# Tile-wise last unit, smaller first loads and later weight splits in a fused two-layer graph kernel

## Chip, cores and metric

The kernel runs on one NeuronCore of a Trainium2 chip. The metric is the device time of one execution in microseconds. Lower is better. Names of engines: PE is TensorE, DVE is VectorE, ACT is ScalarE, POOL is GpSimd, SP is SyncE (here it only issues transfers).

## What is computed

128 graphs of 64 nodes with 384 features pass through two blocks, each followed by a residual sum and a LayerNorm without weights.

```python
x = layernorm(x + attention(x, adj))      # 12 heads of 32; softmax((q k^T)/sqrt(32) + beta*adj), masked where adj <= 0
x = layernorm(x + digcn(x, adj))          # two inner layers l = 0, 1:
#   u = h h^T / sqrt(384);  delta = softmax(u) * adj;  attn = delta / (sum(delta) + 1e-10)
#   ctx = (attn*upper) @ (h Wl + bl) + diag(attn) * (h Ws + bs) + (attn*lower) @ (h Wr + br)
#   h   = relu(layernorm(ctx) * ln_w + ln_b)
```

## The kernel before

**Tiles and units.** A unit is 256 nodes, that is two tiles `t` of 128 nodes, each with two graphs. There are 32 units. Every product with a 384x384 weight is made in three passes of TensorE: both factors are split into a high part (`*_hi`, rounded by ACT) and a low part (`*_lo`, the rest, by DVE or POOL), and `product` (lines 359 to 361) issues high*high, low*high and high*low. So each input of a projection needs two small steps, one on ACT and then one on DVE, before TensorE can start.

**Pipeline.** The program is a loop of steps. In a step three units are in work: EARLY (projections v, q, k and the scores), MID (softmax, attention output, first outer norm, giving `h0` and its transpose `hT`) and LATE (both inner layers). A fourth stage, FINAL, finishes the second inner norm, the sum with `h0` and the last norm of the unit that was LATE one step ago. Each engine has its own instruction list, and the order in it is written out by hand in a `step` function per engine. Engines wait for one another through semaphores only, and each one executes its list in order, so that an instruction that waits holds up everything that is written behind it.

**One LATE unit on PE.** `gram` (u of both tiles), `project_sides` (four projections LEFT and RIGHT for two tiles), `transpose_e`, `project_self` twice, `mix` (the context sums). Layer 0's context is then normalized by DVE, POOL and ACT, and `transpose_z` brings it back for layer 1, which repeats all of it. Between `mix(st, 0)` and `transpose_z` the step puts the EARLY unit's v, q and k projections; between `transpose_z` and `gram(st, 1)` it puts `transpose_probs`, `project_qk(st, 2)` and `attend`. For the last two units there is no EARLY unit left, and for the last one no MID unit either.

**Tile granularity.** In layer 0 and 1 both tiles go together: `make_ctx` writes both tiles' contexts, `stats_inner` takes both tiles' statistics, `inverse_root` on POOL makes both scale factors by one instruction of 128x2, and so on up to `normalize` and the store of a unit's 384 KB of output.

**Beginning.** SP issues x of unit 0 as one load of 384 KB, then three loads of 384 KB with slice m of both w_q and w_k, then the rest. ACT splits x (line 651), then the six weight parts (line 628), DVE the same (lines 830 and 838), and PE makes the three `project_qk`. Until then PE runs ten warm-up products on the identity (line 558). `take_qk` on ACT (lines 660 and 662) moves q and k of a slice out of one PSUM bank; both lie in the same bank. `scores` (line 428) waits for all six. ACT splits the w_v parts between the first and the second `take_qk`.

**Weights of layer 1.** Weights 6, 7 and 8 are split by ACT at the end of `second` (line 641) and by DVE (line 851) in the first step that has a LATE unit: 6 and 7 before `mask_scores`, 8 after `mask_aT`.

## Time and profile before

| what | us |
|---|---|
| median of 3 runs (range) | 1292.63 (1292.51 to 1294.82) |
| the profiled execution | 1295.08 |
| its span, first to last instruction | 1293.4 |
| PE busy in the span | 1261.8 (98%) |
| DVE, ACT, POOL busy | 984.8, 629.7, 366.7 |
| mean granted TensorE clock | 0.990 of full |

The span is 1.7 us shorter than the execution's own time, since it leaves out what lies before the first and after the last instruction. The chain of work that ended last is 96% PE. In the 40 slices of the page PE stands at 9 tenths or more in 36, and is lower in the first and in the last three, which is where the change works.

### The profile page before, as it was taken

How to read it: one execution, taken by the hardware profiler on the slowest of the kernel's cores; microseconds unless marked ns; L12 is line 12 of the kernel's file. 1: busy time of each engine (PE TensorE's matmuls, PEld its weight loads, DVE VectorE, ACT ScalarE, POOL GpSimd, SP SyncE). 2: the span in 40 equal slices, each digit the busy share in tenths (PEclk: the TensorE clock that was granted, in tenths of full speed). 3: DMA queues.
4: the chain of work that ended last, by engine and by line, in shares of the span. 5: the costliest groups of instructions: out<-in, count | busy, mean ns of one | idle time of the engine just before them, and what ended most of it. 6: DMA issues, size and time to landing. Idle time of an engine off the chain costs nothing.

```text
span 1293.4 us, 34503 instructions
## 1 busy us (share of the span) xinstructions
PE 1261.8 (98%) x13844; PEld 1168.9 (90%) x13844; DVE 984.8 (76%) x2672; ACT 629.7 (49%) x1329; POOL 366.7 (28%) x398
## 2 busy tenths in 40 slices
PE   8999999999999999999999999999999999999885
PEld 8999999999999999999999999999999999999774
DVE  5777778777778777878777878777878777787765
ACT  5544554544554544554534554445545445545432
POOL 3222323322323232323222323222323222323211
PEclk9999999999999999999999999999999999999997
DMA  8211111011110111110111110111110111110000
GB/s 273 82 40 57 57 57 30 29 56 57 57 57 24 35 56 57 57 57 18 41 57 56 57 57 7 51 57 57 57 49 9 57 57 57 57 35 12 26 13 25
DMA packets 52206, 66.32 MB, mean 51 GB/s; under 512 B 17744, under 2 KB 38352, under 8 KB 51920
## 3 DMA queue, kind: packets, MB, share of 16 engines
q1 hardware_dynamic: 52048, 64.12, 16.3%
q8 instruction: 110, 1.80, 0.6%
q14 instruction: 48, 0.39, 0.1%
HBM read 38.54 MB, written 12.58 MB: 40 GB/s over the span
## 4 chain that ended last, share of the span: by engine, by line
PE 96%; DVE 2%; issue 1%; ACT 1%; POOL 0%; DMA 0%; POOLq 0%; ACTq 0%; SPq 0%; DVEq 0%
PE bank L359 25%; PE bank L361 23%; PE bank L360 23%; PE bank L550 7%; PE bank L462 4%; PE bank L499 4%; PE bank L447 3%; PE bank L428 3%; PE bank L475 2%; PE bank L485 2%; PE bank L530 1%; DMA late<-in_w_qk 0%; DVE ln_six L1012 0%; DVE probs L900 0%; POOL probs L1184 0%
## 5 line engine op out<-in xcount | busy, mean ns | idle before, releaser
L359 PE MATMUL bank<-w_hi,hT_hi 128*128 128x384 f32 x1158 | 405.2, 350 | 1.9 <-DVE hlr L966 1.0
L361 PE MATMUL bank<-w_hi,hT_lo 128*128 128x384 f32 x1158 | 390.3, 337 | 0.0
L360 PE MATMUL bank<-w_lo,hT_hi 128*128 128x384 f32 x1158 | 390.1, 337 | 0.0
L359 PEld LDWEIGHTS bank<-w_hi,hT_hi 128*128 128x128 f32 x1158 | 218.4, 189 | 6.6 <-issue 2.2
L360 PEld LDWEIGHTS bank<-w_lo,hT_hi 128*128 128x128 f32 x1158 | 219.0, 189 | 0.0
L361 PEld LDWEIGHTS bank<-w_hi,hT_lo 128*128 128x128 f32 x1158 | 218.5, 189 | 0.0
L966 DVE TENSOR_TENSOR hlr<-bank,rows 128x384 f32<-128x384 f32 x256 | 142.0, 556 | 79.4 <-PE bank L361 76.6
L1197 POOL TENSOR_TENSOR ln_rstd<-ln_var,minus_half 128x2 f32<-128x2 f32 x128 | 98.7, 771 | 350.6 <-DVE ln_var L1018 131.5
L1184 POOL TENSOR_TENSOR probs<-probs,row_max 128x768 f32<-128x768 f32 x64 | 94.3, 1475 | 275.9 <-DVE row_max L906 275.9
L981 DVE TENSOR_TENSOR late<-bank,rows 128x384 f32<-128x384 f32 x128 | 71.3, 557 | 123.5 <-PE bank L361 123.5
L359 PE MATMUL bank<-xT_hi,w_hi 128*128 128x256 f32 x558 | 158.8, 285 | 0.0
L360 PE MATMUL bank<-xT_lo,w_hi 128*128 128x256 f32 x558 | 156.1, 280 | 0.0
L361 PE MATMUL bank<-xT_hi,w_lo 128*128 128x256 f32 x558 | 155.9, 279 | 0.0
L722 ACT ACTIVATE late<-late,diag 128x384 f32<-128x384 f32 x64 | 39.5, 618 | 225.4 <-DVE late L981 225.4
L1161 POOL TENSOR_TENSOR xT_lo<-xT_in,xT_hi 128x768 fp32r<-128x768 f32 x31 | 57.6, 1857 | 229.6 <-ACT xT_hi L651 229.6
L715 ACT ACTIVATE e_di<-bank,u_bias 128x128 f32<-128x128 f32 x128 | 45.9, 363 | 132.8 <-DVE u_bias L945 132.8
L361 PEld LDWEIGHTS bank<-xT_hi,w_lo 128*128 128x128 f32 x558 | 106.2, 190 | 0.0
L359 PEld LDWEIGHTS bank<-xT_hi,w_hi 128*128 128x128 f32 x558 | 104.8, 188 | 0.1
L360 PEld LDWEIGHTS bank<-xT_lo,w_hi 128*128 128x128 f32 x558 | 104.9, 188 | 0.0
L550 PE MATMUL bank<-hlr,aT 64*64 64x386 f32 x1024 | 97.8, 497 | 0.0
L730 ACT ACTIVATE late<-late,diag 64x384 f32<-64x384 f32 x128 | 78.4, 613 | 36.1 <-DVE late L981 30.4
L737 ACT ACTIVATE h<-h,ln_shift,ln_rstd 128x384 f32<-128x384 f32 x64 | 41.9, 702 | 99.7 <-DVE ln_shift L866 99.7
(101 smaller groups left out, 2349.0 us busy)
## 6 DMA issues: line engine op xcount, KB each, us to landing
v_halves<-v_stage SPq DMA_DIRECT2D x128, 99.0 KB, 2.3
xT_in<-in_xT SPq DMA_DIRECT2D x32, 384.0 KB, 3.5
x_in<-in_x SPq DMA_DIRECT2D x32, 384.0 KB, 4.1
out<-late SPq DMA_DIRECT2D x32, 384.0 KB, 2.4
late<-in_w SPq DMA_DIRECT2D x7, 576.0 KB, 5.7
adj_in<-in_adj SPq DMA_DIRECT2D x32, 96.0 KB, 3.9
adjT_in<-in_adjT SPq DMA_DIRECT2D x64, 48.0 KB, 3.2
rows<-in_vectors SPq DMA_DIRECT2D x1, 1536.0 KB, 8.0
```

The source lines that it names most:

```text
L359: nc.tensor.matmul(o, l_hi, r_hi, start=first and n == 0, stop=False)
L360: nc.tensor.matmul(o, l_hi, r_lo, start=False, stop=False)
L361: done = nc.tensor.matmul(o, l_lo, r_hi, start=False, stop=final and n == last)
L462: done = nc.tensor.matmul(o[g * N:(g + 1) * N, h:h + 3:2, :], pT[:, t * PAIRS + j, g * N:(g + 1) * N], v[:, :, j, :], start=True, stop=True)
L499: done = nc.tensor.matmul(U_BANK[l][g * N:(g + 1) * N, t * N:(t + 1) * N], a, a, start=kc == 0, stop=kc == KC - 1)
L550: done = nc.tensor.matmul(CTX_BANKS[l][t][o * N:(o + 1) * N, 0:MW], aT[rows_of, t, m, rows_of], hlr[rows_of, t, m, 0:MW], start=m == LEFT, ...
L730: nc.scalar.activation(self_turned[o * N:(o + 1) * N], h_self[rows_of, 1], ACT.Copy, scale=diag[rows_of, 1:2]).then_inc(self_scaled, 1)
L966: nc.vector.tensor_tensor(hlr[:, t, m, 0:D], HLR_BANKS[l][2 * t + m][:, 0:D], bias_row[l][m], ALU.add).then_inc(hlr_ready, 1)
L981: nc.vector.tensor_tensor(h_self[:, t], SELF_BANKS[l][t][:, 0:D], bias_row[l][SELF], ALU.add).then_inc(self_ready, 1)
L1161: nc.gpsimd.tensor_tensor(xT_lo[:, :, :], xT_in[:, slot], xT_hi[:, :, :].bitcast(F32), ALU.subtract).then_inc(xlo_ready, 1)
L1184: nc.gpsimd.tensor_tensor(s, s, row_max[:, t * H:(t + 1) * H].unsqueeze(2).to_broadcast([P, H, N]), ALU.subtract).then_inc(s_shifted, 1)
L1197: nc.gpsimd.tensor_tensor(rstd[:, :], var[:, :], minus_half[:, :], ALU.pow).then_inc(s_rstd, 1)
```

## The change

It has three parts, and two buffers that they need.

1. Beginning. x of unit 0 is loaded in three loads of 128 KB, w_q and w_k in six of 192 KB. The first of the six is issued from ACT's queue, the other eight loads from SP's. ACT and DVE split each part as it lands, in the order x0, q0, x1, x2, k0, q1, k1, q2, k2. PE's first q product waits for one third of x at a time. k of the last slice goes to bank 6 instead of sharing bank 3 with q, and `take_qk` waits for q and for k apart. The split of w_v moves behind the second `take_qk`.
2. Weights 6, 7 and 8. On ACT their splits move from the end of `second` into the next step, behind `exp_gram`, and x's split stands between 7 and 8. On DVE they move behind `mask_scores`: 6 ahead of the third and 7 ahead of the fourth `sides_bias`. This is a move in the first step with a LATE unit alone.
3. The last two units get orders of their own. `next_to_last` puts `transpose_probs` and `attend` ahead of `transpose_z` on PE, and rearranges DVE, ACT and POOL. `last` handles unit 31 tile by tile: own PSUM banks, tile-wise normalization, transposes, split in pieces of 128x128, gram, statistics, POOL factors, last norm and store; its FINAL stage is in the same step. Two changes of storage make it possible: `h0` has three slots instead of two, and the layer 1 context has two buffers instead of one.

The order on ACT at the start, before (hT_hi is the high part of x here, late holds the raw weights, 3x128 elements is one weight part, qT and kT are the `take_qk` moves):

```order
L651 ACT_TABLE_LOAD
L651 ACTIVATE hT_hi<-xT_in 128x768
L628 ACTIVATE w_hi<-late 128x3x128 x6
L637 ACTIVATE columns<-columns 128x3
L660 ACTIVATE qT<-bank,columns 128x256
L662 ACTIVATE kT<-bank,columns 128x256
L633 ACTIVATE w_hi<-late 128x384 x3
L660 ACTIVATE qT<-bank,columns 128x256
L662 ACTIVATE kT<-bank,columns 128x256
L660 ACTIVATE qT<-bank,columns 128x256
L662 ACTIVATE kT<-bank,columns 128x256
```

and the same engine and place after:

```order
L837 ACTIVATE hT_hi<-xT_in 128x256
L843 ACTIVATE w_hi<-late 128x3x128
L837 ACTIVATE hT_hi<-xT_in 128x256 x2
L843 ACTIVATE w_hi<-late 128x3x128
L852 ACTIVATE columns<-columns 128x3
L843 ACTIVATE w_hi<-late 128x3x128 x2
L877 ACTIVATE qT<-bank,columns 128x256
L880 ACTIVATE kT<-bank,columns 128x256
L843 ACTIVATE w_hi<-late 128x3x128 x2
L877 ACTIVATE qT<-bank,columns 128x256
L880 ACTIVATE kT<-bank,columns 128x256
L848 ACTIVATE w_hi<-late 128x384 x3
```

The x split is in three, the weight parts stand between the moves, and the three splits of w_v (the last row) have moved behind the second pair of moves; the third pair follows.

On PE in the step of unit 30, from the layer 0 `mix` (hlr, aT) to the layer 1 `gram` (hT), before, with `transpose_z` as the row from late and the attention rows probs and v_halves:

```order
L550 MATMUL bank<-hlr,aT 64x386 x8
L485 MATMUL bank<-ident,late 128x128 x6
L447 MATMUL bank<-ident,probs 128x128 x12
L462 MATMUL bank<-v_halves,pT 64x2x33 x24
L499 MATMUL bank<-hT 64x64 x12
```

and after:

```order
L623 MATMUL bank<-hlr,aT 64x386 x8
L517 MATMUL bank<-ident,probs 128x128 x12
L532 MATMUL bank<-v_halves,pT 64x2x33 x24
L555 MATMUL bank<-ident,late 128x128 x6
L569 MATMUL bank<-hT 64x64 x12
```

The attention of unit 31 has moved ahead of the transposes of z.

The end of DVE's list, behind the last context of tile 1, before:

```order
L1008 SCALAR_TENSOR_TENSOR den_sq<-den 128x2
L1012 BN_STATS ln_six<-late 128x6 x2
L1015 BN_AGGR ln_mv<-ln_six 128x2 x2
L1018 TENSOR_TENSOR ln_var<-ln_mv,den_sq 128x2
L1022 SCALAR_TENSOR_TENSOR late<-late,ln_mv,rows 128x384 x2
L1027 SCALAR_TENSOR_TENSOR late<-late,ln_rstd,rows 128x384 x2
L1034 SCALAR_TENSOR_TENSOR late<-late,h 128x384 x2
L858 BN_STATS ln_six<-late 128x6 x2
L861 BN_AGGR ln_mv<-ln_six 128x2 x2
L1038 TENSOR_SCALAR ln_var<-ln_mv 128x2
L866 SCALAR_TENSOR_TENSOR ln_shift<-ln_mv,ln_rstd 128x2
```

and after:

```order
L1470 SCALAR_TENSOR_TENSOR den_sq<-den 128x1
L1473 BN_STATS ln_six<-late 128x6
L1475 BN_AGGR ln_mv<-ln_six 128x2
L1478 TENSOR_TENSOR ln_var<-ln_mv,den_sq 128x1
L1363 SCALAR_TENSOR_TENSOR late<-late,ln_mv,rows 128x384
L1489 SCALAR_TENSOR_TENSOR ln_shift<-ln_mv,ln_rstd 128x1
L1373 SCALAR_TENSOR_TENSOR late<-late,ln_rstd,rows 128x384
L1379 SCALAR_TENSOR_TENSOR late<-late,h 128x384
L1530 BN_STATS ln_six<-late 128x6
L1532 BN_AGGR ln_mv<-ln_six 128x2
L1534 TENSOR_SCALAR ln_var<-ln_mv 128x1
L1489 SCALAR_TENSOR_TENSOR ln_shift<-ln_mv,ln_rstd 128x1
```

The same steps stand there for one tile instead of two; those of tile 0 are now written ahead of this, between the layer 1 steps of tile 1. DVE's whole list is 41 rows longer than before.

The diff, cut to what is spoken of:

```diff
-        h0 = sb("h0", [P, 2, T, D])
+        h0 = sb("h0", [P, 3, T, D])
...
-        c1 = late[:, 4 * D:6 * D].rearrange("p (t d) -> p t d", t=T)
+        c1 = [late[:, at:at + 2 * D].rearrange("p (t d) -> p t d", t=T) for at in (4 * D, 7 * D)]
...
-            sp.dma_start(xT_in[:, 0], xT[0]).then_inc(xT_loaded[0], 16)
+            for kc in range(KC):
+                sp.dma_start(xT_in[:, 0, kc], xT[0, :, kc]).then_inc(x0_in[kc] if kc < KC - 1 else xT_loaded[0], 16)
             for m in range(KC):
-                sp.dma_start(qk_raw[:, m], w_qk[m]).then_inc(qk_raw_in[m], 16)
+                for n in range(2):
+                    if (m, n) == (0, 0):
+
+                        continue
+                    sp.dma_start(qk_raw[:, m, n], w_qk[m, :, n]).then_inc(qk_raw_in[m][n], 16)
...
+                if st.has(FINAL) and st.unit(FINAL) == LAST:
+                    for t in range(T):
+                        need(sp, y_ready, st.count(FINAL, 2, t + 1))
+                        sp.dma_start(out[LAST][:, t], context(LAST, 1)[:, t]).then_inc(y_stored[LAST % 2], 16)
...
+                    o = qk_bank(unit, m)[:, 0:TOK] if n == 0 else k_psum(unit, m)
+                    for kc in range(KC):
+                        if unit == 0 and m == 0 and n == 0:
+
+                            last = kc == KC - 1
+                            pe.wait_ge(xhi_ready if last else x0_hi_set, 1 if last else kc + 1)
+                            pe.wait_ge(xlo_ready if last else x0_lo_set, 1 if last else kc + 1)
+                        done = product(o, [(weight(wn, kc, m * P, (m + 1) * P), (hi[:, kc, :], lo[:, kc, :]))],
+                                       first=kc == 0, final=kc == KC - 1)
+                    if unit == 0 and m == KC - 1 and n == 0:
+                        done.then_inc(q0_psum, 1)
...
+            def next_to_last(st):
+                gram(st, 0)
+                project_sides(st, 0)
+                transpose_e(st, 0)
+                project_self(st, 0, 0)
+                project_self(st, 0, 1)
+                mix(st, 0)
+                transpose_probs(st)
+                attend(st)
+                transpose_z(st)
+                gram(st, 1)
+                project_side(st, 1, 0, LEFT)
+                project_side(st, 1, 0, RIGHT)
+                project_side(st, 1, 1, LEFT)
+                transpose_h(st)
+                project_side(st, 1, 1, RIGHT)
+                transpose_e(st, 1)
+                project_self(st, 1, 0)
+                project_self(st, 1, 1)
+                mix(st, 1)
...
+            def last_left_and_gram(st, t):
+                if t == 0:
+                    need(pe, ctx_ready[1], st.count(FINAL, 2, 1))
+                else:
+                    need(pe, hlr_ready, st.count(LATE, 8, 5))
+                for kc in range(KC):
+                    need(pe, z_hi, KC * t + kc + 1)
+                    need(pe, z_lo, KC * t + kc + 1)
+                    done = product(LAST_HLR_BANKS[1][2 * t + LEFT][:, 0:D],
+                                   [((hT_hi[:, t, kc, :], hT_lo[:, t, kc, :]), weight(W_LATE + 3 + LEFT, kc))],
+                                   first=kc == 0, final=kc == KC - 1)
+                    if kc == 0:
+                        last_gram(st, t)
+                done.then_inc(hlr_psum, 1)
...
+            def last(st):
+                gram(st, 0)
+                last_side(st, 0, 0, LEFT)
+                last_side(st, 0, 0, RIGHT)
+                transpose_e(st, 0)
+                last_self(st, 0, 0)
+                last_mix(st, 0, 0)
+                last_side(st, 0, 1, LEFT)
+                last_side(st, 0, 1, RIGHT)
+                last_self(st, 0, 1)
+                last_transpose_z(st, 0)
+                last_mix(st, 0, 1)
+                last_left_and_gram(st, 0)
+                last_side(st, 1, 0, RIGHT)
+                last_transpose_e(st, 0)
+                last_self(st, 1, 0)
+                last_transpose_z(st, 1)
+                last_mix(st, 1, 0)
+                last_left_and_gram(st, 1)
+                last_side(st, 1, 1, RIGHT)
+                last_transpose_e(st, 1)
+                last_self(st, 1, 1)
+                last_mix(st, 1, 1)
...
+            act.dma_start(qk_raw[:, 0, 0], w_qk[0, :, 0]).then_inc(qk_raw_in[0][0], 16)
+
             def begin(st):
-                split_x(st)
-                split_qk_weights()
+                split_x0(0)
+                split_qk_weight(0, 0)
+                split_x0(1)
+                split_x0(2)
+                split_qk_weight(0, 1)
                 scale_bq()
+                split_qk_weight(1, 0)
+                split_qk_weight(1, 1)
                 take_qk(st, 0)
+                split_qk_weight(2, 0)
+                split_qk_weight(2, 1)
+                take_qk(st, 1)
                 split_v_weight()
-                take_qk(st, 1)
                 take_qk(st, 2)
...
                 split_hT(st)
-                split_weight(6)
-                split_weight(7)
-                split_weight(8)
...
+            def last_take_z(st, t):
+                act.wait_ge(z_psum, t + 1)
+                need(act, u_psum, st.count(LATE, 2, 1))
+                need(act, hTlo_ready, st.count(LATE, 4, 2))
+                need(act, self_psum, st.count(LATE, 4, t + 1))
+                for kc in range(KC):
+                    nc.scalar.activation(hT[:, t, kc, :], LAST_Z_BANKS[t][:, kc * P:(kc + 1) * P], ACT.Relu,
+                                         bias=b0_col[:, kc:kc + 1], scale=g0_col[:, kc:kc + 1]).then_inc(z_taken, 1)
+                    act.wait_ge(z_taken, KC * t + kc + 1)
+                    nc.scalar.activation(hT_hi[:, t, kc, :], hT[:, t, kc, :], ACT.Copy).then_inc(z_hi, 1)
...
+                if late and st.unit(LATE) == 0:
+                    exp_gram(st, 0)
+                    split_weight(6)
+                    split_weight(7)
                     split_x(st)
-                if late:
+                    split_weight(8)
+                    scale_self(st, 0)
+                    scale_turned(st, 0)
+                elif early:
+                    split_x(st)
+                if late and st.unit(LATE) != 0:
...
+            def last(st):
+                end = Step(st.s + 1)
+                make_ctx(st, FINAL, 1)
+                max_gram(st, 0)
+                stats_inner(st, FINAL, 1, ln3_den, ln3_stats, ln3_aggr, ln3_eps, ln3_six, ln3_mv, ln3_var)
+                sides_bias(st, 0, 0, LEFT)
+                take_diag(st, 0)
+                sides_bias(st, 0, 0, RIGHT)
+                mask_aT(st, 0)
+                final_center(st, 0)
+                self_bias_tile(st, 0, 0)
+                final_center(st, 1)
+                final_scale(st, 0)
+                need(dve, dz_ready, st.count(LATE, 2, 1))
+                make_ctx_first(st, LATE, 0)
+                last_z_stats(st, 0)
+                sides_bias(st, 0, 1, LEFT)
+                final_scale(st, 1)
+                last_shift(st, 0, ln1_mv, ln1_rstd, ln1_shift, z_rs, z_sh)
+                final_add(st, 0)
+                sides_bias(st, 0, 1, RIGHT)
+                final_add(st, 1)
+                self_bias_tile(st, 0, 1)
+                last_low(st, 0)
+                last_max(st, 0)
+                make_ctx_second(st, LATE, 0)
+                last_z_stats(st, 1)
+                sides_bias(st, 1, 0, LEFT)
+                last_diag(st, 0)
+                last_shift(st, 1, ln1_mv, ln1_rstd, ln1_shift, z_rs, z_sh)
+                sides_bias(st, 1, 0, RIGHT)
+                last_mask_aT(st, 0)
+                final_stats(st)
+                self_bias_tile(st, 1, 0)
+                last_low(st, 1)
+                shift(st, FINAL, ln2_mv, ln2_rstd, ln2_shift, ln2_rs, ln2_sh)
+                dve.wait_ge(tile_dz, 1)
+                make_ctx_first(st, LATE, 1)
+                last_end_stats(st, 0)
+                sides_bias(st, 1, 1, LEFT)
+                last_max(st, 1)
+                final_center(end, 0)
+                sides_bias(st, 1, 1, RIGHT)
+                last_diag(st, 1)
+                final_scale(end, 0)
+                last_mask_aT(st, 1)
+                self_bias_tile(st, 1, 1)
+                final_add(end, 0)
+                last_sum_stats(end, 0)
+                dve.wait_ge(tile_dz, 2)
+                make_ctx_second(st, LATE, 1)
+                last_end_stats(st, 1)
+                final_center(end, 1)
+                last_shift(end, 0, ln2_mv, ln2_rstd, ln2_shift, y_rs, y_sh)
+                final_scale(end, 1)
+                final_add(end, 1)
+                last_sum_stats(end, 1)
+                last_shift(end, 1, ln2_mv, ln2_rstd, ln2_shift, y_rs, y_sh)
...
-                if st.unit(LATE) == 0:
-                    split_weight(6)
-                    split_weight(7)
                 if mid:
                     mask_scores(st, 0, 4)
                 if late:
                     sides_bias(st, 0, 0, LEFT)
                     take_diag(st, 0)
                     sides_bias(st, 0, 0, RIGHT)
+                    if st.unit(LATE) == 0:
+                        split_weight(6)
                     sides_bias(st, 0, 1, LEFT)
+                    if st.unit(LATE) == 0:
+                        split_weight(7)
...
+            def last(st):
+                inverse_root(st, FINAL, 1, 1, ln3_eps, ln3_var, ln3_rstd, ln3_rs)
+                last_inverse_root(0, z_eps, ln1_var, ln1_rstd, z_rs)
+                last_inverse_root(1, z_eps, ln1_var, ln1_rstd, z_rs)
+                inverse_root(st, FINAL, 1, 1, ln2_eps, ln2_var, ln2_rstd, ln2_rs)
+                last_inverse_root(0, end_eps, ln3_var, ln3_rstd, end_rs)
+                need(pool, y_ready, st.count(FINAL, 2, 2))
+                last_inverse_root(0, y_eps, ln2_var, ln2_rstd, y_rs)
+                last_inverse_root(1, end_eps, ln3_var, ln3_rstd, end_rs)
+                last_inverse_root(1, y_eps, ln2_var, ln2_rstd, y_rs)
```

## Rows read from the trace of the kernel before

**Rows 1.** Windows: the steady part (columns in the first line).
```profile
core 0: us, PE busy (x) PEld busy (x) DVE busy (x) ACT busy (x) POOL busy (x), PEclk, DMA share, GB/s
54.30:1206.00 1151.70, 1151.66 (x12810) 1069.13 (x12812) 888.15 (x2433) 570.34 (x1216) 334.57 (x354) 1.00 0.16 47
```

**Rows 2.** Waits: who waited for whom: us, times, longest.
```profile
PE bank L485 <- ACT late L743: 11.1, 2, 5.5
...
PE bank L499 <- ACT hT L697: 1.2, 1, 1.2
...
PE bank L359 <- DVE w_lo L838: 1.0, 1, 1.0
PE bank L359 <- DVE hlr L966: 1.0, 1, 1.0
```

**Rows 3.** Timeline of the beginning: start us, us, engine line, operation [idle before <-releaser].
```profile
1.58 4.23 PE L558 MATMUL bank<-ident 128*128 128x128 f32 x20 [1.58 <-POOL ident L1143]
...
5.53 0.94 ACT L628 ACTIVATE w_hi<-late 128x384 fp32r<-128x384 f32 x2 [0.62 <-DMA late<-in_w_qk]
...
6.86 0.36 PE L359 MATMUL bank<-hT_hi,w_hi 128*128 128x256 f32 x1 [1.04 <-DVE w_lo L838]
...
7.90 1.92 ACT L628 ACTIVATE w_hi<-late 128x384 fp32r<-128x384 f32 x4 [1.44 <-DMA late<-in_w_qk]
...
10.67 1.35 ACT L633 ACTIVATE w_hi<-late 128x384 fp32r<-128x384 f32 x3
...
13.75 0.47 ACT L660 ACTIVATE qT<-bank,columns 128x256 f32<-128x256 f32 x1 [1.00 <-PE bank L361]
...
14.64 1.31 PE L428 MATMUL bank<-kT,qT 32*64 32x64 f32 x96 [0.93 <-ACT kT L662]
```

**Rows 4.** Windows of the beginning, columns as in rows 1.
```profile
3.00:4.00 1.00, 1.00 (x7) 1.00 (x6) 0.00 (x0) 0.00 (x0) 1.00 (x3) 1.00 0.96 356
```

**Rows 5.** Timeline of the first step with a LATE unit.
```profile
36.15 2.63 DVE L851 TENSOR_TENSOR w_lo<-late,w_hi 128x1152 fp32r<-128x1152 f32 x2
...
42.55 1.47 DVE L966 TENSOR_TENSOR hlr<-bank,rows 128x384 f32<-128x384 f32 x3
```

**Rows 6.** The chain that ended last, around layer 0's mix in that step.
```profile
43.24 0.41 PE bank L359
...
46.60 1.46 PE bank L550 x16
```

**Rows 7.** Timeline of PE in the step of unit 30.
```profile
1225.04 1.51 PE L485 MATMUL bank<-ident,late 128*128 128x128 f32 x6 [5.54 <-ACT late L743]
1226.34 2.77 PE L447 MATMUL bank<-ident,probs 128*128 128x128 f32 x12
...
1231.22 0.86 PE L499 MATMUL bank<-hT 128*64 128x64 f32 x24
```

**Rows 8.** Windows of the step of unit 30 and of unit 31 to the end.
```profile
1219.50:1232.10 12.60, 7.06 (x91) 6.69 (x91) 11.52 (x36) 7.45 (x13) 5.32 (x5) 0.73 0.01 2
...
1243.90:1256.10 12.20, 12.19 (x100) 10.80 (x96) 6.60 (x18) 2.75 (x8) 0.00 (x0) 1.00 0.00 1
1256.10:1268.00 11.90, 4.27 (x34) 3.75 (x35) 10.32 (x34) 4.36 (x9) 2.62 (x3) 0.72 0.00 0
1268.00:1280.30 12.30, 12.27 (x70) 10.96 (x68) 4.58 (x10) 3.21 (x9) 0.00 (x0) 0.85 0.08 32
1280.30:1293.40 13.10, 0.00 (x0) 0.00 (x0) 7.57 (x23) 1.75 (x3) 1.69 (x2) 0.69 0.08 31
```

**Rows 9.** Timeline of the last 11 us.
```profile
1282.29 1.01 DVE L1012 BATCH_NORM_STATS2 ln_six<-late 128x6 f32<-128x384 f32 x2
...
1288.40 0.69 POOL L1197 TENSOR_TENSOR ln_rstd<-ln_var,minus_half 128x2 f32<-128x2 f32 x1 [3.61 <-DVE ln_var L1038]
...
1289.33 1.30 ACT L737 ACTIVATE late<-late,ln_shift,ln_rstd 128x384 f32<-128x384 f32 x2 [8.58 <-DVE ln_shift L866]
```

519 lines of the change are left out of this document (426 added, 93 removed).

## The prediction, made before the changed kernel was run

> **What bounds the kernel now.** I read the page's slices first, then the windows, the waits and the timelines of the two ends. Between 54.3 and 1206.0 us TensorE is busy for 1151.66 of 1151.70 us, at the full clock [rows 1]. Nothing on another engine can be gained or won back there, and the change gives PE no less work in it. What is left is the beginning and the last 87 us. The list of PE's waits names the same places: twice 5.5 us for the normalized z of layer 0, once each in the last two units, then 1.2 us for the transposed z, and about 1 us each at the first projection and at one `hlr` [rows 2]. Behind the last product there are 13.1 us without PE at all [rows 8].
>
> The reader should also see the granted clock. In the windows that hold the two 5.5 us gaps it is 0.73 and 0.72 instead of 1.00, and in the one behind the second gap 0.85 [rows 8]: it falls to 1.2 GHz in the course of the gap and comes back to 2.4 GHz only after PE has been busy again for some us. Six transposes then take 1.51 us [rows 7], and the 12 probs transposes behind them 2.77 us. So each of these gaps costs more than its 5.5 us.
>
> **Part A, the beginning.** Before, the first real product starts at 6.86 and the scores at 14.64 [rows 3]. Two things hold the start. One is the data: the raw weights let ACT start at 5.53, and high and low part take 0.5 us each. The other is the warm-up, which keeps PE until 1.58 + 4.23 = 5.81 and is not changed. So with w_q's part landed early the start can move to 5.85 at best: 1.0 us. From there PE has 54 products of 128x256 at about 0.114 us, 6.2 us, against 6.9 between 6.86 and 13.75. The end of k would be at 12.05 if no part came late. I take 12.2, since ACT has to interleave six weight parts at 1.92/4 = 0.48 us with two pairs of q/k moves at 0.84, and the second wait of ACT for data ends at 7.90, with half of the bytes still to come [rows 3]. Behind it the move of q used to start when k was ready, 0.93 us before the scores could go; with k in its own bank q's move hides behind k's products, and 0.5 remains. But the three w_v splits, 1.35 us [rows 3], now stand between the second pair of moves (until about 10.8) and q's last move. If w_v lands where it did, at or before 10.67, they end at 12.2 and q's move at 12.6, k's at 13.1. Scores at 13.1: A = 1.5 us. Bounds: nothing, or a loss of 0.5 if small loads land late, and 2.0 if no load is late. What follows in that step (mask, maximum, POOL's subtraction, exp) is a serial chain that I expect to shift as a whole; weights 3 and 4, issued once all six parts are split, come only 0 to 0.5 us earlier, yet ACT needs them well ahead of the exp that stands behind them.
>
> In a DMA-bound stretch smaller loads can't help: the engines are 0.96 busy at 3 to 4 us [rows 4], moving 356 GB/s. The Trainium skill says so too (DMA: Bandwidth & Descriptors, section Issuing engines are not separate DMA queues): a second issuing queue only saves issue time, as all transfers run on the same 16 engines. By that rule the ACT queue brings w_q no bandwidth, only the place ahead of the row, and A would be what the order of arrival gives, or nothing. That is rival 2.
>
> **Part B, weights 6 to 8.** DVE's two splits of 2.63 us stand at 36.15 ahead of the mask, so the second to fourth `hlr` come from 42.55 on [rows 5] and PE waits 1.0 us for the second [rows 2], then starts `project_self` at 43.24 [rows 6]. With both behind it, that `hlr` is ready by 40.0 and the wait goes: 1.0 us, plus 0.1 of restart. What is late next: `mix` needs the fourth `hlr` and `aT`, now behind splits 6 and 7. Counted from 36.15: mask 1.95, `hlr` 0.5, diagonal 0.8, `hlr` 0.5, split 1.3, `hlr` 0.5, split 1.3, `hlr` 0.5, `aT` 0.7 gives 44.2, while PE comes to `mix` at 45.5 (46.60 before, less 1.1 [rows 6]). Not late. On ACT exp_gram now stands ahead of the splits, x's split 1 us later, and v's projection that needs it follows `mix` at 47. B = 1.1 us, bounds 0 and 1.3.
>
> **Part C, the step of unit 30.** Its z gap was filled with nothing, while probs and attention stood behind it. They come forward into the gap: 12 transposes 1.3 and attention 1.55 at the full clock. Their input is ready if exp is done when `mix` ends at 1219.5; DVE's new list puts both maxima ahead of `aT`, and POOL's 1.5 and ACT's 0.85 follow, so about 1216.3. PE then runs 1219.5 to 1220.8, waits 0.4 for the moves of pT (ACT is at the turned self part until 1220.0), and attention ends at 1222.8. z comes at 1224.7, 0.3 earlier than before, since one maximum has left the chain. Transposes of z 0.65, three moves of 0.49, split 0.5, low part 0.57 on DVE: the layer 1 sides start at 1228.1. Before, gram started at 1231.22 [rows 7] and the sides at 1232.1. That is 4.0, of which 2.7 is the slow clock that is not there (1225.04 to 1231.22 is 6.2 us [rows 7], for 0.65 + 1.3 + 1.55 at the full clock): no idle stretch is longer than 2 us now, and it fell only in gaps of over 4. Against it stands `transpose_h`, whose chain (heads, POOL 2.0, statistics, POOL 0.7, ACT 1.3) is now only 0.4 late. C = 3.5 us. Bounds: 2.0, if the clock falls after all and the attention alone is hidden, and 4.5.
>
> **Part D, unit 31.** Before, from the end of the last mix of unit 30 (1243.9) to the end of the span are 49.5 us [rows 8]: 36.4 with PE and 13.1 without. Of the 36.4, 28.7 are busy (12.19 + 4.27 + 12.27) and 7.7 waits (5.5, 1.2, and 0.9 for the low part of z). The work at the full clock is 25: 12 projections of 1.56 (two of them and a restart are the 3.36 us between the two rows of the chain), two mixes of 1.46 [rows 6], and 3.4 for grams and transposes. So 3.7 is slow clock.
>
> After, with tile 1's layer 0 work placed in tile 0's gap, I follow the lists instruction by instruction, DVE at 0.48 to 0.6 per 128x384 instruction. PE waits for DVE or ACT in seven places: 0.5 at mix of tile 0 (`aT`), 0.4 at z of tile 0, 0.6 for its first split piece and gram, 0.8 at z of tile 1, 1.6 for that tile's first low piece (behind it stand `final_stats` of unit 30, 1.5, and a bias add, on DVE), 0.7 at the last mix, 0.4 for the rest. That is 5.0, so 30.0 instead of 36.4 to the last product. The tail: 1.55 from there to tile 1's context (DVE has still tile 0's sum and statistics, ACT the turned self part 1.25), then context 0.6, statistics 0.95, POOL and hand-over 0.8, scale 0.65, add 0.6, statistics 0.95, POOL 0.8 [rows 9], shift 0.2, ACT 0.7 for one tile of the 1.30, store and end 2.4 instead of 2.8 (half the bytes). That is 10.2 instead of 13.1. D = 49.5 - 40.2 = 9.3, and I take 9.0. Bounds: 4, if each hand-over to PE comes half a us later than counted, and 11.5, if only half of the 5.0 appear.
>
> **Sum.** 1.5 + 1.1 + 3.5 + 9.0 = 15.1. The profiled execution took 1295.08, of which 1293.4 is its span: after, span 1278.3, execution 1280.0. The runs' median is 2.45 under the profiled one, so the forecast is 1292.63 - 15.1 = 1277.5.
>
> **Rivals.**
> 1. VectorE paces the last unit. Speaks for it: it was busy for 6.60 + 10.32 + 4.58 + 7.57 = 29.1 us of the 49.5 [rows 8], has 41 instructions more in all, and now 40 us for it. 41 at the 0.08 us by which the smallest ones follow each other are 3.3, so it is busy for 32 of 40, and every late handover goes straight to PE. Against: the additions are mostly 128x1. Price: nine handovers 0.55 later, 5 us: 1282.5. By a rule of the Trainium skill (VectorE: DVE Perf Modes, section on SBUF-source operations paying a fixed extra latency per instruction) many small tiles pay the fixed part each time, 58 cycles at 0.96 GHz; that would be an estimate of 2.5 us for the 41, and the same rival.
> 2. The start gives nothing: data are the limit, or w_v lands later and holds q's last move. For: rows 4. Against: the first parts only need 320 KB, not 768. A = 0: 1279.0.
> 3. The clock falls in spite of the shorter gaps in the last units: 2.7 + 3.7 come back: 1283.9. Against: no stretch of idleness over 2 us.
> 4. Slower: the steady part pays. PE has no slack there [rows 1], and `h0` and the context now go round three and two buffers, DVE's list for those 29 steps otherwise being the same. If an add or a statistic there became so slow that PE waits in every step, 0.6 us x 29.5 = 17.7, the total is 1295.2. It decides from 15.1/29.5 = 0.51 us per step. Against: the same instructions in the same order, DVE busy for only 888 of 1152 us [rows 1], and one wait (for the store) less.
> 5. The change doesn't do what it says; the lists show that the instructions moved, so hardly.
>
> **How the numbers follow.** Forecast 0.60, rival 1 0.18, rival 2 0.14, rival 3 0.05, rival 4 0.02, rival 5 0.01. The forecast's own range is 1275 to 1280; with rivals 1 and 2 and the bounds of D it is 1274.0 to 1283.0. Less than 0.2% (2.6 us) can't be told from no change here. Faster 0.97, within 0.01, slower 0.02.
>
> **What would show it.** A: first product at 5.85, scores near 13.1. B: no wait for `hlr` at the first `project_self`. C: probs transposes right behind mix, clock 1.00 through that step, its end 3.5 us closer to its beginning. D: 40 us from the last mix of unit 30 to the end, 10.2 of them behind the last product, the largest PE wait at tile 1's low part. The steady part still with PE full. I am wrong if PE's waits in unit 31 add up to 8 or more, if the clock is below 1 there, or if the scores start after 14.

## The result, and the profile after

The changed kernel takes 1282.53 us (median of 4 runs, 1281.19 to 1283.22), before takes 1292.64 (4 runs beside them): ratio 0.9917, 95% interval 0.9899 to 0.9934. That is 10.1 us less, where 15.1 were forecast: inside the range of 1274.0 to 1283.0, close to its upper end, and outside the 1275 to 1280 that the forecast had without its rivals. The predicted time was 5.0 us too low. The profiled execution took 1282.98, its span is 1281.2.

The waits of TensorE after, longest first (who waited for whom: us in total, times, longest), which answer to [rows 2]:

```profile
PE bank L555 <- ACT late L969: 2.3, 1, 2.3
...
PE bank L569 <- ACT hT L918: 1.4, 1, 1.4
...
PE bank L623 <- DVE aT L1300: 0.5, 1, 0.5
...
PE bank L745 <- issue: 0.3, 1, 0.3
PE bank L420 <- ACT hT_hi L1048: 0.2, 1, 0.2
```

The two waits of 5.5 us are gone. One wait of 2.3 for z is left, in the step of unit 30. The last two rows are all that TensorE waits for in unit 31. The windows that answer to [rows 8], of us 1225 to 1233 in the step of unit 30, then of unit 31 (columns as in [rows 1]):

```profile
1225.00:1226.00 1.00, 0.00 (x0) 0.00 (x0) 1.00 (x1) 1.00 (x3) 0.70 (x1) 0.68 0.07 16
1226.00:1227.00 1.00, 0.70 (x13) 0.70 (x14) 0.13 (x2) 0.89 (x3) 0.00 (x0) 0.50 0.00 0
...
1232.00:1233.00 1.00, 1.00 (x6) 1.00 (x6) 0.00 (x0) 0.00 (x0) 0.00 (x0) 0.91 0.00 0
...
1242.00:1250.00 8.00, 8.00 (x67) 6.43 (x64) 7.49 (x25) 3.35 (x8) 0.69 (x1) 1.00 0.13 51
1250.00:1260.00 10.00, 10.00 (x67) 8.50 (x66) 7.62 (x26) 4.48 (x11) 0.55 (x1) 1.00 0.00 1
1260.00:1271.80 11.80, 11.35 (x71) 8.04 (x70) 10.82 (x37) 6.01 (x14) 1.79 (x3) 1.00 0.09 35
1271.80:1281.20 9.40, 0.00 (x0) 0.00 (x0) 4.90 (x17) 1.58 (x3) 1.94 (x3) 0.75 0.11 42
```

Read the third number from the right, the granted clock. In unit 31 it is 1.00 to the last product, where before had 0.72 and 0.85. In the step of unit 30 it still falls to 0.50, which is 1.2 GHz, from 1225.4 to 1232.2. TensorE in that step, answering to [rows 7] (start us, us, [idle before <- releaser]):

```profile
1220.10 1.62 PE L532 MATMUL bank<-v_halves,pT 128*64 128x66 f32 x48 [0.45 <-ACT pT L891]
1224.05 0.85 PE L555 MATMUL bank<-ident,late 128*128 128x128 f32 x6 [2.32 <-ACT late L969]
1226.30 1.55 PE L569 MATMUL bank<-hT 128*64 128x64 f32 x24 [1.41 <-ACT hT L918]
1234.73 1.06 PE L545 MATMUL bank<-ident,h 128*128 128x128 f32 x6
```

Attention (L532) is in the gap, as forecast, and layer 1's gram (L569) comes 3.6 us earlier than before, counted from layer 0's gram of the same step (20.28 us behind it instead of 23.89). But it takes 1.55 instead of 0.86, and the products behind it run at half speed.

The beginning of the changed kernel, ScalarE and TensorE, answering to [rows 3], and then VectorE, GpSimd and TensorE in the first step with a LATE unit, answering to [rows 5, 6]:

```profile
5.88 0.56 PE L420 MATMUL bank<-hT_hi,w_hi 128*128 128x256 f32 x1
8.86 0.47 ACT L877 ACTIVATE qT<-bank,columns 128x256 f32<-128x256 f32 x1 [1.09 <-PE bank L422]
...
9.59 0.94 ACT L843 ACTIVATE w_hi<-late 128x384 fp32r<-128x384 f32 x2
...
13.78 1.25 PE L498 MATMUL bank<-kT,qT 32*64 32x64 f32 x96 [0.56 <-ACT kT L880]
...
38.99 1.88 POOL L1704 TENSOR_TENSOR xT_lo<-xT_in,xT_hi 128x768 fp32r<-128x768 f32 x1 [8.47 <-ACT xT_hi L865]
39.11 2.98 DVE L1173 TENSOR_TENSOR w_lo<-late,w_hi 128x1152 fp32r<-128x1152 f32 x1
...
40.84 1.72 POOL L1714 TENSOR_TENSOR adj_diag<-adj_in,diag_sel 128x192 f32<-128x192 f32 x1
42.48 1.34 DVE L1173 TENSOR_TENSOR w_lo<-late,w_hi 128x1152 fp32r<-128x1152 f32 x1
...
45.03 1.53 PE L623 MATMUL bank<-hlr,aT 64*64 64x386 f32 x16 [0.55 <-DVE aT L1300]
```

The first product starts at 5.88 (forecast 5.85), the scores at 13.78 (13.1). Of two equal low parts on VectorE one takes 1.34 us and the other 2.98; mix then waits for aT, a wait that the forecast did not have.

A table of the two profiled executions puts the stretches side by side. "Step of unit 30" is from layer 0's gram of unit 30 to that of unit 31. The gains add up to the 12.2 us between the two spans, 2.1 more than between the medians; the profiled execution of before took 1295.08, which is 2.4 above the median of before.

| stretch | before | after | gain | forecast |
|---|---|---|---|---|
| A: start to scores | 14.64 | 13.78 | 0.9 | 1.5 |
| B and the steady part: scores to the gram of unit 30 | 1192.69 | 1192.24 | 0.4 | 1.1 |
| C: step of unit 30 | 36.59 | 36.06 | 0.5 | 3.5 |
| D: unit 31 to the end | 49.5 | 39.1 | 10.4 | 9.0 |

### The profile page after: what moved, and what is told of

The parts are those of the page before. It is cut to its first block, busy times and chain, and to the rows that moved or that the text cites. A ratio compares the mean times of both kernels' runs of the same rounds, so it can differ in the third digit from the quotient of the medians.

```text
span 1281.2 us, 34717 instructions
## 1 busy us (share of the span) xinstructions
PE 1263.4 (99%) x13844; PEld 1166.7 (91%) x13844; DVE 990.4 (77%) x2691; ACT 632.6 (49%) x1338; POOL 370.6 (29%) x401
## 4 chain that ended last, share of the span: by engine, by line
PE 97%; DVE 1%; issue 1%; ACT 1%; POOL 0%; POOLq 0%; DVEq 0%; ACTq 0%
PE bank L420 25%; PE bank L422 23%; PE bank L421 23%; PE bank L623 7%; PE bank L569 4%; PE bank L532 4%; PE bank L517 3%; PE bank L498 3%; PE bank L545 2%; PE bank L555 2%; PE bank L603 1%; PE bank L631 0%; DVE probs L1222 0%; POOL probs L1727 0%; PE bank L745 0%
## 5 line engine op out<-in xcount | busy, mean ns | idle before, releaser
L623 PE MATMUL bank<-hlr,aT 64*64 64x386 f32 x992 | 94.7, 497 | 0.5 <-DVE aT L1300 0.5
```

Source lines behind the costliest of these rows:

```text
L623: done = nc.tensor.matmul(CTX_BANKS[l][t][o * N:(o + 1) * N, 0:MW], aT[rows_of, t, m, rows_of], hlr[rows_of, t, m, 0:MW], start=m == LEFT, ...
```

## The experiments

Each ran beside the kernel before on its own chip, so ratios are compared, and stretches within the traces. 1 us is 0.0008 of the ratio.

### Part C undone

```
-                if st.unit(MID) == UNITS - 1:
-                    next_to_last(st)
-                    return
```
(on all four engines)

> The changed kernel with part C alone undone: the step of unit 30 is issued by the general list again, the beginning, weights 6 to 8 and unit 31 stay changed. Theory: part C gave only 0.5 us, since the granted clock fell although the idle stretches became shorter, so this kernel is within 1 us of the changed one: ratio to before 0.9920, about 1282.9, span of a run at the profiled one's clock 1281.7. Rival (the forecast's C of 3.5 was right, and the 5 us are missing elsewhere): 3.5 us slower than changed, about 1286, ratio 0.9948. In the trace the stretch from the end of layer 0's mix to the gram of layer 1 of unit 30 should be as in the kernel before, with a wait of 5.5 us.

Measured: 1283.60 us (4 runs), ratio 0.9919 (0.9906 to 0.9933), against 0.9917 with part C. The step of unit 30 took 35.86 us, less than the 36.06 with part C. So part C as built gained nothing that these runs can tell, and the rival of 1286 us fell. The trace of this run, TensorE and windows:

```profile
1224.05 1.52 PE L555 MATMUL bank<-ident,late 128*128 128x128 f32 x6 [5.54 <-ACT late L966]
...
1228.05 1.62 PE L532 MATMUL bank<-v_halves,pT 128*64 128x66 f32 x48
```

```profile
1220.00:1221.00 1.00, 0.00 (x0) 0.00 (x0) 1.00 (x4) 0.84 (x1) 0.06 (x1) 0.89 0.00 0
...
1227.00:1228.00 1.00, 0.93 (x6) 0.69 (x4) 1.00 (x3) 0.82 (x3) 0.00 (x0) 0.70 0.00 0
```

The gap is the same 5.54 us as in [rows 7], but the clock fell 2.3 us into it (at 1220.8; the gap begins at 1218.5) and was back at 1227.6, ahead of attention, which took 1.62. In before, by its windows, it fell 4.3 us into the gap, was back at 1230.6, and attention took 2.34 still. In a second trace of before (e12_before_again) it fell 3.8 us into the gap and was back at 1228.5. So where in a gap the clock falls differs from one execution to the next. The step took 35.86, 36.37 and 36.59 us, shortest where the clock fell earliest; that the 0.7 us are the clock's alone isn't shown, since the shortest is of another kernel.

### Idle matmuls in the gaps of unit 30

```
+            def fill(n):
+                for _ in range(n):
+                    nc.tensor.matmul(bank[2][:, 0:P], ident[:, :], ident[:, :], start=True, stop=True)
                 attend(st)
+                fill(9)
                 transpose_z(st)
+                fill(5)
                 gram(st, 1)
```

> The changed kernel with 14 more matmuls of the identity, whose results nobody reads, on TensorE in the step of unit 30: 9 ahead of the transposes of z and 5 ahead of layer 1's gram, 0.21 us each at the full clock, 3.0 us in all, in the place of 3.7 us of idleness. Theory (the clock ate part C): the granted clock stays at 1.00 from 1219 to 1245, layer 1's gram still starts at about 1226.3, lasts 0.65 instead of 1.55, the projection products behind it run at 0.17 instead of 0.32 each, and the end comes 2.5 us earlier: 1280.0, ratio 0.9898. Rival (the chain of h on VectorE holds the step): the clock is full, but TensorE then waits for h at its transposes, and the total stays within 0.5 us of the changed kernel's 1282.5.

Measured: 1281.11 us (4 runs), ratio 0.9900 (0.9885 to 0.9915), against the changed kernel's 0.9917: 2.2 us less. The step of unit 30 took 33.93 instead of 36.06. The intervals of the two ratios overlap, so it is the traces that carry this reading. The windows and TensorE's rows:

```profile
1225.00:1232.00 7.00, 6.24 (x60) 5.94 (x59) 5.67 (x14) 3.22 (x9) 2.14 (x2) 1.00 0.00 0
```

```profile
1224.54 0.85 PE L555 MATMUL bank<-ident,late 128*128 128x128 f32 x6
1225.22 1.28 PE L652 MATMUL bank<-ident 128*128 128x128 f32 x10
1226.79 0.92 PE L569 MATMUL bank<-hT 128*64 128x64 f32 x24 [0.29 <-ACT hT L924]
1228.18 0.41 PE L420 MATMUL bank<-w_hi,hT_hi 128*128 128x384 f32 x1 [0.47 <-DVE hT_lo L1268]
...
1233.09 1.06 PE L545 MATMUL bank<-ident,h 128*128 128x128 f32 x6
```

Not one transfer or result comes earlier here; only the clock is kept, and the transposes of h (L545) wait for nothing. The rival, h's chain on VectorE, falls. The Trainium skill (TensorE: Matmul & The Clock Gate, part 1 on the clock gate) has the same picture, activity releases the throttle; this pair of traces agrees, 1.00 against 0.50.

### One of the two gaps filled

`fill(9)` alone, and `fill(5)` alone.

> As e2_fill, but with only the 9 idle matmuls ahead of the transposes of z; the 1.41 us gap ahead of layer 1's gram stays empty. Theory A (the fall comes from the two gaps together): the clock stays at 1.00, and nearly all of the 2.1 us of e2_fill is kept, total ratio about 0.990. Theory B (a single gap of 1.4 us is enough for the fall): the granted clock is 0.5 in some us behind layer 1's gram, and the total lies at 0.991 to 0.992.

> As e2_fill, but with only the 5 idle matmuls ahead of layer 1's gram; the 2.32 us gap ahead of the transposes of z stays empty. Theory A (the fall comes from the two gaps together): the clock stays at 1.00, total ratio about 0.990. Theory B (the 2.3 us gap alone makes it fall): the idle matmuls and the gram run at 0.5 as in the changed kernel, total ratio 0.992, perhaps 0.3 us worse since the idle matmuls take twice their time.

Measured: 1281.82 us and ratio 0.9908 with the 2.3 us gap filled, 1281.46 and 0.9906 with the 1.4 us gap filled (intervals of 0.003 overlap). The traces tell them apart. Windows of the first:

```profile
1227.00:1228.00 1.00, 0.53 (x17) 0.42 (x13) 0.78 (x2) 0.53 (x2) 0.00 (x0) 1.00 0.00 0
1228.00:1229.00 1.00, 1.00 (x5) 1.00 (x6) 0.96 (x4) 0.31 (x2) 0.00 (x0) 0.75 0.00 0
1229.00:1230.00 1.00, 1.00 (x5) 1.00 (x4) 0.97 (x6) 0.50 (x4) 0.00 (x0) 0.50 0.00 0
```

and of the second:

```profile
1226.00:1227.00 1.00, 0.71 (x21) 0.62 (x22) 0.21 (x1) 0.89 (x3) 0.00 (x0) 1.00 0.00 0
...
1228.00:1229.00 1.00, 1.00 (x7) 1.00 (x7) 0.97 (x5) 0.47 (x3) 0.00 (x0) 1.00 0.00 0
```

With only the 1.41 us gap (and 0.47 behind the gram) the clock fell all the same, at 1228.5, behind both, and for a shorter time (until 1231.1): the step took 35.50. With only the 2.32 us gap it stayed at 1.00, and the step took 33.94. So in these two traces the longer gap alone did no harm and the shorter one did: the length of the longest gap does not decide. These are single traces; as the moment of the fall differs between executions, I don't claim that either gap would always do the same.

The record has one number for every execution, traced or not, that bears on this: the mean granted clock of the whole span. An estimate from the changed kernel's trace: 7 us at half the clock in 1281 lower it by 0.0027. With both gaps filled it is 0.998, 0.997, 0.997 and 0.998, with the 2.3 us gap filled 0.997 four times, and with the 1.4 us gap filled 0.998, 0.998, 0.997 and 0.996, the last two in the two longest executions. The unedited changed kernel has 0.995 or 0.996 in seven of its nine executions and 0.998 in two, which are the shortest of their sets (1281.19 and 1281.94 us). So the fall behind the two gaps seems frequent and not certain, and the 2.3 us gap alone is not shown to be safe.

### The kernel before with idle matmuls

24 of them ahead of `transpose_z` in the steps of units 30 and 31, behind a wait for the masked scores, whose bank they may write then.

> The kernel before, with 24 matmuls of the identity (5.1 us at the full clock), whose results nobody reads, in each of the two 5.5 us gaps ahead of the transposes of z of units 30 and 31. Nothing else is changed, so it gives what the clock alone takes there. By the working of the forecast the two slow stretches cost 2.7 and 3.7 us: 6.4 less than before, 1286.2, ratio 0.9951. Rival: products that come faster only wait longer for the other engines' chains (h in the one, low part and hlr in the other), and less than 2 us are won: 1290.7 or more.

Measured: 1292.74 us (11 runs) against 1293.59, ratio 0.9991 (0.9982 to 1.0000). About 1.2 us by the ratio, where the forecast's working put 6.4 on the clock. What ended the waits now:

```profile
1228.13 1.63 PE L462 MATMUL bank<-v_halves,pT 128*64 128x66 f32 x48 [1.17 <-ACT pT L680]
...
1262.27 0.92 PE L499 MATMUL bank<-hT 128*64 128x64 f32 x24 [1.41 <-ACT hT L704]
1265.17 0.66 PE L359 MATMUL bank<-w_hi,hT_hi 128*128 128x384 f32 x1 [1.99 <-DVE hT_lo L944]
```

Faster transposes only reach the next wait sooner, for pT and for the low part, and behind the waits of 1.41 and 1.99 the clock of unit 31 falls after all (0.32 us from product to product instead of 0.17), though for less time: from 1264.8 to 1268.2, where before had 1261.3 to 1271.6. In unit 30 it stayed at 1.00. Counted in the traces, the step of unit 30 is 1.4 and unit 31 0.8 us shorter than in the first trace of before, 1.2 and 0.6 shorter than in the second. So here a slow clock cost far less than its slow instructions add up to, since other waits stood behind them. The step of unit 30 took 35.21 here against 33.93 in the changed list with idle matmuls: with the clock kept in both, part C's order (attention in the gap, and the order of the other engines that goes with it) is worth 1.3 us.

### Part D undone

```
-        LAST = UNITS - 1
+        LAST = 1000
```
(so that no unit is the last one, and the end waits for whole stores)

> The changed kernel with part D alone undone: unit 31 and its end are issued by the general list again (in whole units, not tile by tile), the beginning, weights 6 to 8 and the step of unit 30 stay changed. Theory: D is 10.3 of the 12.2 us by which the profiled spans differ, so only some 1.5 us stay: 1291.0, ratio 0.9987. Rival (the forecast's sizes: D 9.0 and the rest 6.1): 1286.5 for this kernel, ratio 0.9953.

Measured: 1292.66 us (11 runs), ratio 0.9991 (0.9982 to 1.0000). Unit 31 takes 49.2 us again. All that is not part D is worth 1.2 us by the ratio, with an interval of 0 to 2.3; part D is worth 0.0074, 9.6 us by the ratio and 10.1 by the traces.

### The order of splits and moves at the beginning

```
+                split_qk_weight(2, 0)
+                split_qk_weight(2, 1)
                 take_qk(st, 0)
-                split_qk_weight(2, 0)
-                split_qk_weight(2, 1)
                 take_qk(st, 1)
```

> The changed kernel with ScalarE's two last weight parts (q and k, part 2) split ahead of its first moves of q and k instead of behind them. In the changed kernel ScalarE stood idle for 1.09 us ahead of these moves, and TensorE then waited 0.28 us for the split part. Theory: the parts have landed by then, so they are split in the idle time, that wait goes and k is ready 0.3 us earlier; the scores start 0.3 us earlier against the first product. Rival (the data had not landed): ScalarE waits for a DMA at that place, its moves of q and k come later, and the scores don't start earlier. The total can't tell 0.3 us; the trace does.

Measured: 1282.69 us, ratio 0.9915 (0.9900 to 0.9930). The parts had landed, the 0.28 us wait is gone, and the scores start at 13.96, no earlier. ScalarE's row:

```profile
7.65 1.77 ACT L843 ACTIVATE w_hi<-late 128x384 fp32r<-128x384 f32 x3 [0.24 <-DMA late<-in_w_qk]
```

So the theory was right on the data and the wait, and wrong on what follows. ScalarE's first moves came at 9.32 instead of 8.86, behind the two splits. Its second pair came at 11.10 instead of 10.84, as it waited for TensorE, whose products were later too: at the start six of them stood 0.21 us or more apart instead of four (0.25 us in all), and behind them three products took 0.353 us instead of 0.34, of which the trace shows no cause.

### A shorter warm-up

`PREWARM = 5` instead of 10.

> The changed kernel with 5 warm-up matmuls instead of 10. In the changed kernel the first product starts at 5.88, when the warm-up ends, though its parts are ready at 5.3. Theory (data pace the beginning, the warm-up hides only the wait for them): the first product starts at 5.3 to 5.4, but x's later parts, the weight parts and the slow clock take that back, and the scores start within 0.3 us of the 13.7 to 14.2 seen so far. Rival (the warm-up was the limit): the scores start 0.5 us earlier, below 13.5. If the granted clock comes back later as well, it is a loss of up to 1 us.

Measured: 1284.58 us (4 runs), ratio 0.9931 (0.9917 to 0.9945), a loss of 1.7 us. TensorE's rows:

```profile
5.47 0.55 PE L420 MATMUL bank<-hT_hi,w_hi 128*128 128x256 f32 x1 [1.39 <-DVE w_lo L1160]
...
7.74 0.41 PE L421 MATMUL bank<-hT_lo,w_hi 128*128 128x256 f32 x1
...
15.51 1.25 PE L498 MATMUL bank<-kT,qT 32*64 32x64 f32 x96 [0.86 <-ACT kT L880]
```

The first product starts 0.4 us earlier, and products are still slow at 7.7 (0.41 each, 0.28 with the long warm-up from 6.8 on). The first 28 start 0.21 us apart, until 11.4, and those behind them 0.11 to 0.12 apart. The loss is larger than the 1 us that was expected at most. Two products 0.21 us apart with 256 columns each are 1.2 GHz by an estimate from these rows, yet the profile's column has 1.00 there:

```profile
7.00:8.00 1.00, 1.00 (x7) 1.00 (x7) 0.50 (x1) 0.14 (x1) 0.00 (x0) 1.00 1.06 301
```

In no trace of this case does this column show the slow products of the start (1.00 from 1.6 to 15 us in all); there one has to go by the time from product to product. In this kernel the warm-up matmuls that held up the first product were worth more than the time they took.

### GpSimd waits for two low parts

```
+                if st.unit(LATE) == 0:
+                    pool.wait_ge(w_lo_set, 5)
                 if early and not st.unit(EARLY) == 0:
                     split_x(st)
```

> The changed kernel, but in the step of the first unit in layer 0's projections GpSimd starts only when VectorE has made the low parts of weights 6 and 7. Theory (the two engines hold each other up when both work in SBUF): both low parts take 1.34 us, none 2.98, GpSimd's diagonal and side selections take 0.6 and 0.5 instead of 1.7 each wherever no VectorE split runs beside them, and mix starts 0.5 us earlier against the gram of its step, without the 0.55 us wait for aT. Rival (that low part is slow for another reason, such as the reading of late while a DMA writes it): it takes 2.98 us again, and GpSimd's instructions 1.7.

Measured: 1282.08 us (4 runs), ratio 0.9910 (0.9895 to 0.9925). VectorE, GpSimd and TensorE:

```profile
39.22 1.35 DVE L1173 TENSOR_TENSOR w_lo<-late,w_hi 128x1152 fp32r<-128x1152 f32 x1
...
42.38 1.88 POOL L1704 TENSOR_TENSOR xT_lo<-xT_in,xT_hi 128x768 fp32r<-128x768 f32 x1 [11.74 <-DVE w_lo L1173]
43.28 2.19 DVE L1173 TENSOR_TENSOR w_lo<-late,w_hi 128x1152 fp32r<-128x1152 f32 x1
44.20 1.73 POOL L1714 TENSOR_TENSOR adj_diag<-adj_in,diag_sel 128x192 f32<-128x192 f32 x1
...
44.64 1.53 PE L623 MATMUL bank<-hlr,aT 64*64 64x386 f32 x16
```

The low parts of weights 6 and 7 take 1.35 each, mix waits for nothing and starts 0.52 us earlier behind its gram, and layer 0's probs transposes come another 0.3 earlier; at the gram of unit 30 0.4 of the 0.8 is left (1191.80 us from the scores, against 1192.24). The slow spot has moved with GpSimd, to the low part of weight 8 (2.19). The ends show how they meet: x's low part ends at 44.26, weight 8's low part at 45.47, 1.21 later, a little under its own 1.35; the diagonal ends at 45.93, 0.46 later again. So one waits for the end of the other, and they do not share. The Trainium skill says this (SBUF — State Buffer, section Who interferes with whom): a VectorE instruction with two SBUF inputs and a GpSimd instruction that reads SBUF contend for one port pair, and the later one is blocked until the first ends. These traces agree.

### A second look at the kernel before

> The kernel before, unedited, for a second trace of its own. The nine traces of the changed beginning start the scores at 13.66 to 14.20, so the place of one execution says little to a quarter of a us; the kernel before has 14.64 and, with the idle matmuls of e3_before_fill, 15.45. Expected: scores at 14.5 to 15.5; in the step of the first unit in layer 0's projections VectorE's product for the diagonal takes 0.28 or 0.74 us, by whether GpSimd's selections run beside it, and TensorE waits 0.2 or 1.0 us for the second hlr to match; in the gap of unit 30 the granted clock falls at another moment than before's 1223.9.

Measured: 1293.15 us (one run). The scores start at 13.81, not at 14.5 or later: this expectation was wrong, and with it the reading that part A has a sure 0.9 us. The granted clock fell at another moment, as expected (1221.6). VectorE's product for the diagonal takes 0.49, neither of the two values expected, and TensorE's wait is 0.19:

```profile
40.14 0.49 DVE L953 TENSOR_TENSOR diag_junk<-e_di,adj_diag 128x128 f32<-128x128 f32 x1
...
41.76 0.41 PE L359 MATMUL bank<-w_hi,hT_hi 128*128 128x384 f32 x1 [0.19 <-DVE hlr L966]
```

In the execution that the forecast was read from, this product and the small one behind it (0.16 in the second trace) had run beside GpSimd's diagonal and one of its side selections:

```profile
41.02 0.74 DVE L953 TENSOR_TENSOR diag_junk<-e_di,adj_diag 128x128 f32<-128x128 f32 x1
...
42.11 0.51 DVE L959 SCALAR_TENSOR_TENSOR dz<-z_di,diag 128x2 f32<-128x2 f32 x1
```

The wait of 0.98 us that part B was to remove is 0.19 and 0.18 in the two other traces of that code. This second execution has a span of 1291.4, 10.2 longer than the changed kernel's: stretch by stretch, it is start to scores 0.0, scores to the gram of unit 30 -0.35, step of unit 30 0.3 (36.37), unit 31 10.2.

### Together, beside the changed kernel unedited

The idle matmuls, GpSimd's wait, and in the step of unit 30:

```
-                final_center(st, 1)
                 shift(st, LATE, ln1_mv, ln1_rstd, ln1_shift, ln1_rs, ln1_sh)
                 heads_out(st)
+                final_center(st, 1)
```

> The changed kernel with three edits: the 9 and 5 idle matmuls of e2_fill, GpSimd's wait of e6_pool_waits, and in the step of unit 30 VectorE's second final_center moved behind the h of both tiles, so that it no longer runs beside GpSimd's inverse root of layer 0's variance. Theory (each loss is its own): 2.1 us of e2_fill plus 0.8 of e6_pool_waits, and the root takes 0.7 instead of 1.0, so that z comes 0.3 earlier; 3.2 us less than the changed kernel on the same chip, ratio to before 0.989. Rival (they overlap, or the root is slow for another reason): the root still takes 1.0, and no more than 2.2 us are won.

> The changed kernel itself, unedited, on the same chip as e9_together. It gives the base of that comparison and a second trace of the changed kernel: the theory of the clock expects again some 7 us at 0.5 behind the two gaps of unit 30, and 36 us from layer 0's gram of unit 30 to that of unit 31; ratio 0.9917.

Measured: 1280.12 us (5 runs, four at 1279.86 to 1280.27 and one at 1285.95, with a mean granted clock of 0.948 where the others have 0.998, which draws the ratio to 0.9908, 0.9891 to 0.9925); the changed kernel on the same chip 1282.82 us, 0.9919 (0.9906 to 0.9933). That is 2.7 us between the medians, 13.1 under before; but the intervals of the ratios overlap. The spans of the two traces differ by 2.7 as well, though this execution's scores started 0.4 later (14.20 against 13.76); behind the scores it is 3.1, 0.7 up to the gram of unit 30 and 2.4 in its step (33.63 against 36.02). That is near the 3.2 of the theory. GpSimd's root:

```profile
1221.04 0.69 POOL L1746 TENSOR_TENSOR ln_rstd<-ln_var,minus_half 128x2 f32<-128x2 f32 x1 [4.61 <-DVE ln_var L1365]
```

It took 1.00 in the changed kernel. The step is 0.3 us shorter than with the idle matmuls alone (33.93). The second trace of the changed kernel repeats the first to 0.1 us, slow clock included.

## Why the prediction was right, and where its sum was not

**Part D carried the result, by a sum with two errors that cancel.** Forecast 9.0, measured 10.1 to 10.4. From the last mix of unit 30 to the last product it takes 29.7 us; 30.0 were counted. But that was 25 of work and 5.0 of waits, and the trace has 29.3 of work and 0.4 of waits. That the two errors are of one size is luck. The hand-overs that I added up one by one don't appear: the largest was to be 1.6 for tile 1's low piece, and is 0.16. And the work is larger, since mix by tiles costs twice:

```profile
L745 PE MATMUL bank<-hlr,aT 64*64 64x386 f32 x32 | 6.1, 496 | 0.3 <-issue 0.3
```

That is TensorE in unit 31: 32 matmul records in four mixes, 6.1 us. In [rows 6] 16 of them take 1.46 together; here 8 take 1.45 (from 1248.14 to the product at 1249.59). So with both tiles in one mix the second tile's matmuls added no time, and alone they take as long as the first's: four mixes instead of two are 2.9 us of the missing work. The other 1.4 is not found in one row; the first product behind each piece starts the next 0.25 to 0.28 us later instead of 0.17, and there are nine such places. The tail behind the last product was 9.4, forecast 10.2. Rival 1 (VectorE paces the unit) did not happen: it is busy for 25.9 of 29.8 us, and TensorE is not held. Its price, 1282.5, is the measured time to the tenth, and that is chance.

**Part C is the step that failed.** "No idle stretch is longer than 2 us now, and it fell only in gaps of over 4": the stretch is 2.3, and the clock fell. 3.5 was forecast, with 2.0 as the lower bound for just this case, and 0.5, 0.3 and -0.2 come out against three traces of the general list. Rival 3 (0.05) happened in this half. With the clock kept the step takes 33.9, 2.7 less than in [rows 7]; so 2.1 of the loss are the clock. Of the remaining 0.8, 0.6 is z, which came 0.3 us later than before and not 0.3 earlier: GpSimd's root for it took 1.00 instead of 0.69, as it ran beside an instruction of VectorE that the new order had put there (e9_together moves that one, and wins 0.3). The rest goes with a wait of 0.47 for the low part. The mistake is one of reading: two gaps of one length show that such a gap is enough, not that a shorter one is safe.

**The price of the clock was too high as well.** 6.4 us were put on it in before; 1.2 came back by the ratio when it was kept in unit 30 and for most of unit 31 (e3_before_fill), as other waits stood right behind.

**Part A: 0.9 in the pair of profiles, forecast 1.5.** The first product is where it was forecast. Nine executions with the changed beginning start the scores at 13.66 to 14.20 (median 13.90), the three of before at 13.81, 14.64 and 15.45. In the three, ScalarE waited 0.62, 1.44 and 2.63 us for a load of the weight parts (0.84 in the first trace of the changed kernel). So no late start was seen with the change, and nothing was gained on the good one; what a median gains, three starts can't say. Rival 2 (nothing gained) is half right.

**Part B: forecast 1.1, measured none to 0.6.** From the scores to the first mix it is 31.25 us after, and 31.89, 31.25 and 31.17 in the three traces of that code before. The 0.98 us wait was mostly the two engines in each other's way, in one execution. The change removed it and put a longer VectorE instruction beside GpSimd, 2.98 for 1.34. Up to the gram of unit 30 the changed kernel is even behind two of the three (1192.24 against 1192.69, 1191.89 and 1191.64).

**The steady part did not move,** so rival 4 fell. Against the second execution of before, whose start is equal to 0.03 us, all 10.2 us are part D's.

## What to carry to other kernels

A gain read from one execution is as sure as the rows around it are repeatable: look whether the wait that goes is the program's or only that execution's (an instruction that is longer than its siblings is the sign). Expect much from idle matmuls in a gap only where no other wait follows closely, and don't take a gap for harmless because it is shorter than those in which the clock fell. When a unit is cut into tiles, check for each TensorE stage whether its tiles ran beside each other; if they did, the stage can cost twice, as mix did here.

## What the hardware showed

- VectorE and GpSimd held each other up for whole instructions: low part 2.98 against 1.34, diagonal 1.72 against 0.60, side selection 1.70 against 0.52, root 1.00 against 0.69. That they block and don't share is read from the ends in e6_pool_waits; that two inputs in SBUF are the condition was not tried.
- The granted clock fell to 0.50 in the second of two idle stretches of 2.3 and 1.4 us with 0.7 us of work between, stayed at 1.00 in the one trace with only the 2.3 left, and fell in the one with only the 1.4 left. By the mean clocks it did not fall in every execution of the changed kernel. What decides is open.
- In one and the same gap of 5.5 us it fell 2.3, 3.8 and 4.3 us into it in three executions.
- At the start products ran 0.21 us apart and the column of the granted clock had 1.00 all the same (e11_short_warmup).
- The mix of one tile (8 matmul records) takes as long as that of two tiles together (16 records), 1.45 us.
- With one and the same beginning (that of before) the scores started at 13.81, 14.64 and 15.45.
